# Expert scores and counting products last in TensorE's slots, and an earlier ranking and scatter of the last quarter of the tokens

## What is computed

```python
xn = layernorm(x)
x = x + long_convolution(xn) + moe_all_experts(xn)     # layer 0
xn = layernorm(x)
x = x + linear_attention(xn) + moe(xn)                 # layer 1

# moe of layer 1: 8 experts, the 2 best of each token
gate_hidden = einsum('nh,erh->ner', xn, W_A)           # R = 64
scores = sqrt(sum(gate_hidden ** 2, -1))
topk_scores, topk_idx = top_k(scores, 2)
w = softmax(topk_scores)
g, up = gate_hidden @ W_B, xn @ W_up                   # F = 256
y = (silu(g) * up) @ W_down                            # for the chosen experts alone
```

## Time and profile before

| | |
|---|---|
| median of 3 runs | 650.4 us (650.07 to 652.51) |
| the profiled execution's own time | 651.89 us |
| its span, first to last instruction | 650.1 us |
| PE busy | 578.5 us, 89% |
| DVE busy | 411.3 us, 63% |
| ACT busy | 308.2 us, 47% |
| POOL busy | 302.5 us, 47% |

### The profile page before, as it was taken

One profiled execution on the slowest core, in us unless ns is written; L12 is line 12 of the kernel. 1 busy time (PEld: TensorE's weight loads), 2 busy tenths in 40 slices (PEclk: granted clock), 3 DMA queues, 4 the chain that ended last, 5 costly groups with the idle time before them and its releaser, 6 DMA issues.

```text
span 650.1 us, 11488 instructions
## 1 busy us (share of the span) xinstructions
PE 578.5 (89%) x3698; PEld 513.3 (79%) x3698; DVE 411.3 (63%) x1089; ACT 308.2 (47%) x566; POOL 302.5 (47%) x297
## 2 busy tenths in 40 slices
PE   4889999999999999999999899998879896799850
PEld 1868998989988899878888798787668685688740
DVE  5885997505432344234455888898868687476776
ACT  3570216465643566244465764765664632354320
POOL 4870020006520455246432468668457577775450
PEclk9997999999999999999999999999999899799995
DMA  6341059999999530233222224203223221332517
GB/s 213 128 210 50 1 162 150 154 151 149 152 153 148 168 122 0 66 76 93 86 83 80 53 77 120 73 23 102 66 60 84 67 67 53 103 87 67 175 38 258
DMA packets 80465, 67.71 MB, mean 104 GB/s; under 512 B 7109, under 2 KB 73222, under 8 KB 79607
## 3 DMA queue, kind: packets, MB, share of 16 engines
q1 hardware_dynamic: 75798, 57.85, 42.4%
q0 software_dynamic: 4320, 8.92, 4.0%
q10 hardware_dynamic: 290, 0.21, 0.1%
HBM read 34.05 MB, written 32.91 MB: 103 GB/s over the span
## 4 chain that ended last, share of the span: by engine, by line
PE 56%; DVE 13%; issue 12%; POOL 11%; ACT 4%; DMA 3%; POOLq 0%; SPq 0%; ACTq 0%; DVEq 0%
PE banks L1681 7%; PE banks L1683 7%; PE banks L1682 7%; PE banks L1792 6%; POOL expert_rows L818 4%; PE banks L1811 4%; PE banks L1899 3%; PE banks L1781 3%; PE banks L2052 2%; PE banks L1766 2%; PE banks L1767 2%; PE banks L1802 2%; POOL arena L848 2%; PE banks L2037 1%; DMA arena<-result_rows 1%
## 5 line engine op out<-in xcount | busy, mean ns | idle before, releaser
L833 POOL DMA_INDIRECT result_rows<-arena x71 | 68.6, 966 | 37.4 <-DVE arena L1555 19.2
L818 POOL DMA_INDIRECT expert_rows<-arena x64 | 63.7, 995 | 26.0 <-issue 17.5
L848 POOL TENSOR_TENSOR arena<-arena 128x512 f32<-128x512 f32 x32 | 42.8, 1338 | 65.1 <-DVE arena L1515 65.0
L1365 DVE TENSOR_TENSOR arena<-banks,arena 128x512 f32<-128x512 f32 x64 | 41.2, 686 | 49.8 <-PE banks L1792 49.2
L788 POOL TENSOR_TENSOR arena<-arena 128x256 f32<-128x256 f32 x32 | 23.3, 728 | 87.0 <-DVE arena L1365 86.8
L1515 DVE TENSOR_TENSOR arena<-banks,arena 128x512 f32<-128x512 f32 x48 | 33.1, 689 | 46.9 <-PE banks L1683 39.6
L1899 PEld LDWEIGHTS banks<-arena 128*128 128x128 f32 x384 | 49.0, 191 | 7.5 <-POOL arena L848 4.0
L1899 PE MATMUL banks<-arena 128*128 128x128 f32 x384 | 51.4, 277 | 2.9 <-POOL arena L848 2.3
L1792 PE MATMUL banks<-arena 128*128 128x128 f32 x384 | 50.9, 276 | 0.7 <-ACT arena L944 0.7
L1093 ACT ACTIVATE arena<-banks 128x512 f32<-128x512 f32 x48 | 28.7, 599 | 47.4 <-PE banks L1683 47.1
L1792 PEld LDWEIGHTS banks<-arena 128*128 128x128 f32 x384 | 46.6, 192 | 1.5 <-ACT arena L944 1.5
(11 more groups left out here) (277 smaller groups left out, 1673.6 us busy)
## 6 DMA issues: line engine op xcount, KB each, us to landing
expert_rows<-arena SPq DMA_DIRECT2D x12, 1430.0 KB, 28.7
arena<-expert_weights SPq DMA_DIRECT2D x64, 128.0 KB, 3.4
arena<-expert_rows SPq DMA_DIRECT2D x71, 65.0 KB
arena<-result_rows SPq DMA_DIRECT2D x8, 512.0 KB, 6.2
arena<-in_x SPq DMA_DIRECT2D x4, 512.0 KB, 7.1
arena<-in_dft_f SPq DMA_DIRECT2D x1, 2048.0 KB, 11.3
normed_hi<-xnt_hi SPq DMA_DIRECT2D x1, 2048.0 KB, 6.7
normed_lo<-xnt_lo SPq DMA_DIRECT2D x1, 2048.0 KB, 11.1
```

What stands on the lines that cost most here:

```text
L818: pool.indirect_dma_start(out=xrows, out_offset=bass.IndirectOffsetOnAxis(ap=SLOT[:, k, t:t + 1], axis=0), in_=XNF[:, t, :], in_offset=Non ...
L833: pool.indirect_dma_start(out=yrows, out_offset=bass.IndirectOffsetOnAxis(ap=DEST[:, i, n:n + 1], axis=0), in_=YB[:, i % YBUFS, n, :], in_ ...
L848: nc.gpsimd.tensor_tensor(out=AM0[slot % 2], in0=AM0[slot % 2], in1=WB0[:, m, :], op=ALU.mult).then_inc(weighted, 1)
L1365: ins = nc.vector.tensor_tensor(out=dst[:, q % 2], in0=xs, in1=h, op=ALU.mult)
```

## The change

Three edits. In every slot of PE, `expert_gates` and `counts` move from their place before the pair's other products to the very end of the slot. For the last quarter the steps are put closer: rank in slots 60, 61, 61, counts in 62, slots in 63, tables in 64 to 67, the scatter from slot 64. The second half of `tables`' part 2 becomes a part 3 of its own; for the first three quarters both lie in the same slot as before. `shares()` is not edited, but gives another list from the new number: the 16 scatters in slots 64 to 69, and the six results that were in slots 64 and 65 after them.

```diff
--- before.py
+++ after.py
@@ -89,11 +89,13 @@
 W_PARTS = 4
 PAIR0 = 52
 SLOTS = PAIR0 + NP + 2
-SCATTER_FROM = (30, 42, 54, 66)
+SCATTER_FROM = (30, 42, 54, 64)
 ROWS_FROM = 54
 SCATTERS = (3, 3, 2, 2, 3, 3)
 COUNT_BANK = (3, 3, 5, 5)
-COUNT_AT = (16, 16, 17, 16)
+COUNT_AT = (16, 16, 17, 14)
+RANK_AT = ((12, 14, 15),) * 3 + ((12, 13, 13),)
+TABLE_AT = ((19, 20, 21, 21),) * 3 + ((16, 17, 18, 19),)
 ARENA_WORDS = 53000
 ARENA_AT = 16640
 Z_AT = 10
@@ -1473,6 +1475,7 @@
                     link(nc.vector.tensor_tensor(out=STEPPED[:, 0:n], in0=FLAG[:, 0:n],
                                                  in1=ROW_STEP.unsqueeze(1).broadcast_to((P, n, 16)), op=ALU.mult))
                     link(nc.vector.tensor_reduce(out=BLOCK_ROWF[:, 0:n], in_=STEPPED[:, 0:n], axis=AX.X, op=ALU.add))
+                if part == 3:
                     link(nc.vector.scalar_tensor_tensor(out=BLOCK_ROWF[:, 0:n], in0=NUMBER[:, 0:n], scalar=float(P),
                                                         in1=BLOCK_ROWF[:, 0:n], op0=ALU.mult, op1=ALU.add))
                     link(nc.vector.tensor_scalar(out=BLOCK_ROWF[:, 0:n], in0=BLOCK_ROWF[:, 0:n],
@@ -1646,14 +1649,14 @@
                     c = due(slot, 9 + t)
                     if c is not None:
                         norm_sum(TPC * c + t)
-                for part, at in enumerate((12, 14, 15)):
-                    bt = odd_due(slot, at)
-                    if bt is not None:
-                        rank(bt, part)
-                for part in range(3):
-                    bt = odd_due(slot, 19 + part)
-                    if bt is not None:
-                        tables(bt, part)
+                for bt in range(NBT):
+                    for part, at in enumerate(RANK_AT[bt]):
+                        if odd_due(slot, at) == bt:
+                            rank(bt, part)
+                for bt in range(NBT):
+                    for part, at in enumerate(TABLE_AT[bt]):
+                        if odd_due(slot, at) == bt:
+                            tables(bt, part)
                 if i in WEIGH_AT:
                     weigh(WEIGH_AT.index(i))
                 if i >= BACK_AT:
@@ -2110,10 +2113,6 @@
                 c = due(slot, 4)
                 if c is not None:
                     turn_normed(c)
-                for t in range(TPC):
-                    c = due(slot, 7 + t)
-                    if c is not None:
-                        expert_gates(TPC * c + t)
                 for h in range(2):
                     c = due(slot, 15 + h)
                     if c is not None:
@@ -2121,9 +2120,6 @@
                 c = query_due(slot, 0)
                 if c is not None:
                     queries(c)
-                for bt, at in enumerate(COUNT_AT):
-                    if odd_due(slot, at) == bt:
-                        counts(bt)
                 if 1 <= i <= NP:
                     turn_products(i - 1)
                 if 1 <= slot <= N0 * NCH:
@@ -2132,6 +2128,13 @@
                     down_rows(i - 2)
                 for n, step in attention_steps(i):
                     attention_step(n, step)
+                for t in range(TPC):
+                    c = due(slot, 7 + t)
+                    if c is not None:
+                        expert_gates(TPC * c + t)
+                for bt, at in enumerate(COUNT_AT):
+                    if odd_due(slot, at) == bt:
+                        counts(bt)
 
 
 _OUT = ((P, T, D), "float32")
```

## The result

The changed kernel took 643.37 us (median of 20 runs, 639.84 to 648.84), the kernel before 650.72 beside it (20 runs, 647.17 to 653.12): a ratio of 0.9899 (95% interval 0.9875 to 0.9923), 7.35 us less. The forecast was 640.9, its range 638.0 to 646.5. The profiled execution took 642.45 by itself, its span is 640.6. In the profile after, a line number is two or three above that of before: L1684 is before's L1681, L850 is L848, L1922 is L1919.

A forecast was written before the change was run, and what follows sets the result against it. PE, busy 89%, bounds the kernel, with idle waits for last-quarter rows and table and half clock behind them. -5.5 - 1.0 - 2.4 - 1.4 + 0.8 = -9.5 gives 642.4 profiled, median 640.9; range 638.0 to 646.5.

The forecast's parts named there:

- the rows and the scatter: Last quarter: first scatter at 520.3 instead of 531.20, rows at 545.5; slot 71's 5.48 wait goes whole, 3.5 to spare.
- some 11: Sign of being right: the last quarter's first scatter comes some 11 us earlier against PE's slots.
- the sum for slots 70 to 72: Waits for rows (5.48) and table (2.44) vanish, and full clock saves 2.4 around slots 70 and 71.
- the packing: Slots 64 to 66: DVE's table work moved closer together delays PE and eats 1.4 of the table's 2.44.
- the table's net: Before `turn_products(17)`: of the 2.44 wait for the table, only 1.0 comes back.
- slots 55 to 57: With transposes ahead of the scores in slot 55, ACT's chain and slot 57 come 1.4 earlier; ends 0 and 3.3.
- the 0.8 for slots 13 to 46: Late scores no longer cover `down0_step`'s waits for POOL in the first 52 slots: 0.8 lost, ends 0 and 2.4.
- the next slot's gate product covers it: Slots 28 and 40: `counts` some 0.8 later delays DVE's `slots` and `product0`; costed at nothing.
- what PE loses early in one is waited for later anyway: First 52 slots: POOL bounds two scatter stretches holding three waits, so only one loss of 0.8 was counted.
- The clock falls elsewhere: Rival: new short waits in slots 64 to 68 bring another stretch at 1.2 GHz, +2.4, 643.3; 7%.
- The roots L870: Rival: POOL's roots beside `product(11)` block DVE; `slot_in` and slot 63 up to 2.9 later, 643.8; 2%.
- Slower: Rival: without scores before it, `down0_step` waits for POOL in all 24 slots, 19.4 in all, 659.5; 2%.

The follow-up runs named there:

- old scatter: Changed kernel, scores and counts late only from slot 52, last quarter's SCATTER_FROM back at 66: ratio 0.9877 with stands; 646.24, 0.9907 without.
- Old tables: Changed kernel with scores and counts late only from slot 52, last quarter's tables back in slots 67 to 69: 695.87, ratio 0.9961, on a chip with stands.
- late from 52: Changed kernel with scores and counts in their old place before slot 52, last in the slot from 52 on: 693.86 with stands, 640.87 without.
- both together: Changed kernel with scores and counts late only from slot 52, and the first two quarters' scatters 2 in each of 8 slots: 641.65, ratio 0.9847.
- Spreading the scatters: Changed kernel with the scatters of the first two quarters put as 2 in each of 8 slots instead of 3, 3, 2, 2, 3, 3: 642.21, ratio 0.9853.
- the quarter alone: Changed kernel with scores and counts back in their old place in every slot: 692.99, ratio 0.9921, then 692.49, 0.9895, both on chips with stands.
- scores alone: Kernel before with only scores and counts moved to the end of TensorE's slots: 702.61, ratio 1.0067, on a chip with stands.

## Why the prediction was right, and where it was wrong

**Right: the rows and the scatter.** `slot_in` was forecast for 520.0, the first scatter for 520.3, the rows for 545.5:

```profile
519.90 0.17 DVE L1429 CAST arena<-arena 128x16 int32<-128x16 f32 x1
...
525.72 0.68 DVE L1539 TENSOR_TENSOR arena<-banks,arena 128x512 f32<-128x512 f32 x1
...
531.30 0.68 DVE L1539 TENSOR_TENSOR arena<-banks,arena 128x512 f32<-128x512 f32 x1
...
535.38 0.68 DVE L1539 TENSOR_TENSOR arena<-banks,arena 128x512 f32<-128x512 f32 x1
```

L1429 ends at 520.07, the first scatter goes at 520.36, the last at 539.72, and with the 6.1 of before the rows are in at 545.8, an estimate. PE asks for them at 547.8, so 2.0 were to spare and not 3.5. (That the absolute times fit so well is part luck: this execution stood 0.95 later than before at slot 63. By slot 64 the scatter came 13.70 after it before and 2.87 now, the "some 11".) The old scatter, 6.5 longer in slots 70 to 72, shows that this edit carried it.

**Right: the sum for slots 70 to 72.** 5.48 + 2.44 + 2.4 of clock is 10.3; it came to 10.4, in five executions of four kernels. Old tables alone cost 4.3 of it (on a chip with the stands), the old scatter alone 6.5, each with a piece of the half clock.

**Right, a size off: the packing.** `product(13)` to `(15)`, forecast for 525.8, 531.3 and 536.0, came at 525.72, 531.30 and 535.38 (the rows above). I had the pile eat 1.4. Slots 65 to 70 show +0.9 to +1.0 in all kernels on ordinary chips, slots 63 to 65 -0.1 to -0.5 where the clock fell there as before (twice it did not, -1.5). So the table's net is 1.5 to 2, not 1.0; with its clock some 3.4, by the old tables. What PE waited for in these slots was not `product` but DVE's step for the attention (L1580): 1.08 and 1.52, where the kernel before waited 0.71 and 0.54 for it.

**Right: slots 55 to 57**, forecast -1.4, seen as -1.5 to -1.6 in all six executions on ordinary chips. But late from 52 and both together then lost 1.1 in slot 57 to the clock, the other three kernels not.

**Wrong: the 0.8 for slots 13 to 46, which came to 6.9.** This is the term that was mis-sized, and the sum would have been -3.4 with it; the rest came out 1.7 to 3.0 better than its parts. Three things failed in the step. First, "at those three the 0.8 of scores no longer runs before the wait but after it", with 24 placements taken as harmless because they never waited. The waits in slots 33 and 45 grew by nearly what I had said (1.23 to 1.87, 0.64 to 1.33; I had counted one of them and not both), but slots 32 and 44, where no wait had shown, lost 0.4 and 0.3 as well: I had counted the waits that were there, and not how near POOL's other products stood. Slots 31 and 43 lost 0.4 each by the step that I had costed at nothing, "the next slot's gate product covers it": `counts` came later, and DVE's `slots` and residual step with it. No run moved `counts` alone, so this rests on the rows above. Slots 31 to 34 lose 2.9 in all, with the half clock behind slot 33's wait, and 43 to 45 1.35. Second, "what PE loses early in one is waited for later anyway": of 6.9 only 0.65 came back, by slot 55. Third, I had put "The clock falls elsewhere" into slots 64 to 68, where it never fell on an ordinary chip, and not behind these very waits, where it fell twice in both executions. In slot 37 a further step was not in the sum at all: with PE 2.9 later, a rank step of DVE fell beside POOL's product and took 2.06 instead of 0.69, for a loss of 2.8 with its clock. (The Trainium skill, SBUF — State Buffer, "Who interferes with whom", says that a VectorE instruction with two SBUF inputs contends with a GpSimd instruction that reads SBUF, that the ports they share are an exclusive lock, and that issue order decides who blocks. This row agrees in length: 0.69 plus the product's 1.27 is 1.96, near the 2.06. It doesn't show the order: DVE's step began 0.23 before POOL's and was the one drawn out. The roots L870, on which I tested this rule, did not hold DVE off.) Spreading the scatters, which moves nothing on PE, brought back 5.4 of the 6.8, and the waits for POOL in slots 32, 33, 44 and 45 went with it; this shows the first cause, though some 1.7 of the 5.4 were waits of the kernel before. The rival "Slower" named the right mechanism for those slots and drew it as all 24 or none; it was four.

**Right by luck: the total.** My forecast for the profiled execution was 642.4 and it took 642.45, but 3.8 of its gain was there before slot 0. The median of 20, 7.35 less, is between the -5.1 to -6.4 of the slots and the 9.5 of the forecast; its interval (5.0 to 8.1) holds the slots' figure. That the median fell into the range with one term off by 6.1 is luck too: the other terms came out 1.7 to 3.0 better, and 1.4 of the 3.0 is the half clock that one execution did without.

**The version that beats both** is late from 52: 640.87 against 645.83 and 652.56 on one chip. On a chip with the stands it took 693.86 and the quarter alone 692.99, no difference in the noise.

## What to carry to other kernels

When work is moved to the end of an engine's list, write down for each place what it was covering and by how little, not only where a wait already shows: on TensorE a bare wait costs its length and, behind some waits of 1.5 us and more, though not behind all (one of 1.87 went without), a stretch of half clock too. A step worth 1.5 in one stage can cost 7 in another, so ask whether a placement has to hold for all stages. And compare executions by stretches between fixed points of the program: here the same kernel starts its slot 30 6 us apart in two executions, and then repeats itself to about 0.1 in every stretch in which the clock does the same.

## What the runs showed of the hardware that was not expected

- On two of the four chips of these experiments PE, ACT and DVE came to two long stands in every kernel profiled (the kernel before has no profile there; its 698 suggests the same), while POOL sent a scatter or a result every 1.27. Both lie within the sixteen scatters of a quarter or just behind them; in the first two quarters, whose scatters have products of POOL between them, there was none. The cause stays open; that scatters run at both is seen, that they are the cause was not tried.
- A wait of 1.87 and one of 2.50 were each followed by a stretch of TensorE at 1.2 GHz, the lower of its two levels, that lasted some 3.4 us (windows with a mean granted clock of 0.53 and 0.57 above); so was one of 1.54 or 1.55 in slot 57 in two kernels, and not in four executions of three others with 1.54 or 1.55. In scores alone the same wait of 1.87 in the same slot was followed by products at full clock. So the length of the wait alone does not decide it.
- One 128x512 step of DVE took 2.06, 1.56 or 1.54 instead of 0.69 beside a POOL product of the same size.
